# Softmax passes of a graph network: one product per tile with three bf16 parts side by side, in place of three products that accumulate

## The reference

```python
logits = leaky_relu(al_s[src] + al_d[dst], 0.2)
m = segment_max(logits, dst)
e = exp(logits - m[dst])
denom = segment_sum(e, dst)
alpha = e / denom[dst]
out = segment_sum(alpha[:, :, None] * xw[src], dst)
```

## Time and profile before

| | |
|---|---|
| median of 3 runs | 10558.96 us (10516.83 to 10563.09) |
| the profiled execution, its own time | 10553.33 us |
| its span, first to last instruction | 10551.6 us |
| mean granted TensorE clock | 0.627 of full speed |
| the three softmax passes lie at about | 4185 to 5770, 5870 to 7420, 7600 to 9010 us |

### The profile page before, as it was taken

One profiled execution on the slowest core, in us unless ns is written; L12 is line 12 of the kernel. 1 busy time (PEld: TensorE's weight loads), 2 busy tenths in 40 slices (PEclk: granted clock), 3 DMA queues, 4 the chain that ended last, 5 costly groups with the idle time before them and its releaser, 6 DMA issues. The chain is left out here.

```text
span 10551.6 us, 128176 instructions
## 1 busy us (share of the span) xinstructions
PE 5587.4 (53%) x36650; PEld 4424.0 (42%) x36651; DVE 3907.8 (37%) x11738; ACT 1797.2 (17%) x4681; POOL 5548.3 (53%) x5840
## 2 busy tenths in 40 slices
PE   3555555555544344665666565666545454545554
PEld 3444554444322222444444344444334443444444
DVE  4333322222311112554555455555444444333323
ACT  1222210100111112111111211111211111111111
POOL 3666656666366563554543454555355555255554
PEclk7555555656666666666667666666655555566665
DMA  3444422333232232433432443443223332233333
GB/s 112 144 143 141 143 69 75 80 78 78 57 75 73 72 74 68 114 112 108 115 110 80 118 113 110 112 113 109 64 79 83 79 82 77 63 97 97 98 96 80
DMA packets 711652, 1000.35 MB, mean 95 GB/s; under 512 B 355976, under 2 KB 397000, under 8 KB 711240
## 3 DMA queue, kind: packets, MB, share of 16 engines
q1 hardware_dynamic: 497816, 538.69, 17.4%
q0 software_dynamic: 213552, 458.86, 17.4%
HBM read 927.44 MB, written 69.60 MB: 94 GB/s over the span
## 5 line engine op out<-in xcount | busy, mean ns | idle before, releaser
L749 POOL DMA_INDIRECT gat_rows<-xw_table,gat_index x2496 | 2357.8, 945 | 2547.2 <-DVE gat_msg_s L1849 1442.7
L1948 PE MATMUL bank<-gat_msg_s,gat_hot 128*128 128x264 f32 (+1 forms) x4992 | 1898.5, 539 | 551.5 <-DVE acc L1870 213.6
L1948 PEld LDWEIGHTS bank<-gat_msg_s,gat_hot 128*128 128x128 f32 x4992 | 1289.7, 299 | 1020.1 <-issue 483.6
L749 POOL DMA_INDIRECT att_rows<-pre_table,att_index x832 | 784.9, 943 | 744.0 <-ACT att_index L739 349.1
L749 POOL DMA_INDIRECT msg_rows<-pre_table,msg_index x832 | 786.3, 945 | 610.8 <-ACT msg_index L739 369.8
L749 POOL DMA_INDIRECT gcn_rows<-x_table,gcn_index x832 | 806.4, 969 | 497.0 <-issue 260.0
L749 POOL DMA_INDIRECT gcn_rows<-in_x,gcn_index x832 | 804.9, 967 | 499.1 <-issue 252.9
L958 PE MATMUL bank<-gcn_rel,gcn_rhot 100*128 100x64 f32 x3328 | 638.9, 344 | 793.6 <-issue 618.4
L798 PE MATMUL bank<-gcn_msg_s,gcn_hot 128*128 128x128 f32 x3328 | 731.8, 373 | 426.9 <-issue 416.6
L958 PEld LDWEIGHTS bank<-gcn_rel,gcn_rhot 100*128 100x128 f32 x3328 | 614.0, 267 | 818.8 <-issue 714.5
L798 PEld LDWEIGHTS bank<-gcn_msg_s,gcn_hot 128*128 128x128 f32 x3328 | 640.3, 276 | 495.8 <-issue 495.7
(11 more groups left out here) (302 smaller groups left out, 8929.5 us busy)
## 6 DMA issues: line engine op xcount, KB each, us to landing
gcn_ids<-rel_rows SPq DMA_DIRECT2D x208, 400.0 KB
gat_hot_half<-edge_hots SPq DMA_DIRECT2D x312, 256.0 KB
gat_dhot<-dst_hots SPq DMA_DIRECT2D x312, 256.0 KB
gcn_dst<-dst_rows SPq DMA_DIRECT2D x104, 512.0 KB
gat_rows<-xw_table,gat_index POOLq DMA_INDIRECT x2496
edge_hots<-gcn_hot_half SPq DMA_DIRECT2D x104, 256.0 KB
dst_hots<-gcn_dhot SPq DMA_DIRECT2D x104, 256.0 KB
gcn_hot_half<-edge_hots SPq DMA_DIRECT2D x104, 256.0 KB
```

The source lines that it names most:

```text
L749: pool.indirect_dma_start(self.rows[n.q][:, j, :], None, self.table, bass.IndirectOffsetOnAxis(ap=self.index[n.q][:, j:j + 1], axis=0))\
L1948: ins = pe.matmul(bank_of(n, g)[:, 0:wide], hot[n.q][:, j, :], msg[q][:, j, :], start=j == n.groups[g].start, stop=j == n.groups[g].stop - 1)
```

## The change

In each softmax step, `pick` and `dst_gather` issue one product per tile instead of three. The three parts stand side by side in the moving operand, so that a product has 27 (pick) or 48 columns (dst_gather) and does not accumulate. The three results lie side by side in PSUM, and VectorE sums them with a `tensor_reduce` each: `found` (192 elements per partition in, 64 out) in `maxima`, and `drow` (384 in, 128 out) in `logits`. Both results now lie in SBUF, where before the sum was read from PSUM. The PSUM banks are free again once these sums are made: `pick` waits for `merged` (the sum of the step before) instead of `offered`, `dst_gather` for `joined` instead of `shifted`. `cut_ends` writes the third part as fp32 with a bf16 value in it, instead of as bf16. Tiles, gathers, loads and the orders of the engines stay.

```diff
-        ends, ends_rest = (ring_sb(st, s, TWO, [P, BATCH, HEADS + 1]) for s in ("ends_s", "ends_rest"))
-        ends_low = ring_sb(st, "ends_low", TWO, [P, BATCH, HEADS + 1], BF16)
+        cuts = ring_sb(st, "ends_s", TWO, [P, BATCH, PARTS, HEADS + 1])
+        ends, ends_rest, ends_low = ([t[:, :, k, :] for t in cuts] for k in range(PARTS))
+        found, merged = ring_sb(st, "found", TWO, [P, BATCH, HEADS]), st.sem("merged")
...
-        drow = row_ps[:, 0:BATCH * 2 * HEADS].rearrange("p (b h) -> p b h", b=BATCH)
+        drow, joined = ring_sb(st, "drow", TWO, [P, BATCH, 2 * HEADS]), st.sem("joined")
...
+        all_upper = lambda t: t.bitcast(BF16).rearrange("p b k (h two) -> p b (k h) two", two=2)[:, :, :, 1]
...
                     dve.wait_ge(picked, n.total(1, RING + 1))
-                    dve.tensor_scalar(pen[q][:, :].unsqueeze(2), view[:, :, HEADS:HEADS + 1], -1.0, -FAR, ALU.add, ALU.mult)\
+                    dve.tensor_scalar(pen[q][:, :].unsqueeze(2), view[:, :, 0, HEADS:HEADS + 1], -1.0, -FAR, ALU.add, ALU.mult)\
                         .then_inc(penal, 1)
+                    dve.tensor_reduce(found[q][:, :, :], view[:, :, :, 0:HEADS].rearrange("p b k h -> p b h k"), AX.X, ALU.add)\
+                        .then_inc(merged, 1)
+                    dve.wait_ge(merged, n.total(1, 1))
                     dve.wait_ge(penal, n.total(1, 1))
-                    dve.tensor_tensor(cand[q][:, :, :], view[:, :, 0:HEADS], spread(pen[q][:, :], HEADS), ALU.add)\
+                    dve.tensor_tensor(cand[q][:, :, :], found[q][:, :, :], spread(pen[q][:, :], HEADS), ALU.add)\
...
                     dve.wait_ge(dst_rows, n.total(1, RING + 1))
-                    dve.tensor_tensor(lg[q][:, :, :], al_s[q][:, :, :], drow[:, :, 0:HEADS], ALU.add)\
+                    dve.tensor_reduce(drow[q][:, :, :], row_ps[:, 0:BATCH * PARTS * 2 * HEADS]
+                                      .rearrange("p (b k h) -> p b h k", b=BATCH, k=PARTS), AX.X, ALU.add).then_inc(joined, 1)
+                    dve.wait_ge(joined, n.total(1, 1))
+                    dve.tensor_tensor(lg[q][:, :, :], al_s[q][:, :, :], drow[q][:, :, 0:HEADS], ALU.add)\
...
-                    pe.wait_ge(offered, n.total(1, 1))
-                    pieces = upper(ends[q][:, :, :]), upper(ends_rest[q][:, :, :]), ends_low[q]
+                    wait_past(pe, merged, n.total(1, 0))
+                    size = PARTS * (HEADS + 1)
+                    pieces = all_upper(cuts[q][:, :, :, :])
                     for j in range(BATCH):
-                        for k, piece in enumerate(pieces):
-                            ins = pe.matmul(pick_ps[:, j * (HEADS + 1):(j + 1) * (HEADS + 1)], hots.half[n.q][:, j, :], piece[:, j, :],
-                                            start=k == 0, stop=k == PARTS - 1)
+                        ins = pe.matmul(pick_ps[:, j * size:(j + 1) * size], hots.half[n.q][:, j, :], pieces[:, j, :],
+                                        start=True, stop=True)
                     ins.then_inc(picked, 1)
...
-                    size = 2 * HEADS
+                    size = PARTS * 2 * HEADS
                     pe.wait_ge(dhot_in[n.q], n.count(16, 16))
                     pe.wait_ge(shown, n.total(1, 1))
                     pe.wait_ge(parted, n.total(1, 1))
-                    pe.wait_ge(shifted, n.total(1, 1))
+                    wait_past(pe, joined, n.total(1, 0))
                     for j in range(BATCH):
-                        for k in range(PARTS):
-                            ins = pe.matmul(row_ps[:, j * size:(j + 1) * size], dhot[n.q][:, j * P:(j + 1) * P],
-                                            parts[q][:, n.group_at[j], k, :], start=k == 0, stop=k == PARTS - 1)
+                        ins = pe.matmul(row_ps[:, j * size:(j + 1) * size], dhot[n.q][:, j * P:(j + 1) * P],
+                                        parts[q][:, n.group_at[j], :, :].rearrange("p k h -> p (k h)"), start=True, stop=True)
                     ins.then_inc(dst_rows, 1)
```

More of the change, by code:

```diff
@@ L1755, in power @@
                     q = n.of(TWO)
-                    act.wait_ge(shifted, n.total(1, 2))
+                    act.wait_ge(shifted, n.total(1, 1))
                     act.wait_ge(msg_made, n.total(1, RING))
@@ L1792, in maxima @@
                     q = n.of(TWO)
-                    view = pick_ps[:, 0:BATCH * (HEADS + 1)].rearrange("p (b h) -> p b h", b=BATCH)
+                    view = pick_ps[:, 0:BATCH * PARTS * (HEADS + 1)].rearrange("p (b k h) -> p b k h", b=BATCH, k=PARTS)
                     first = n.turn is None and n.total(1, 0) == 0
@@ L1841, in logits @@
                     dve.wait_ge(leaky, n.total(1, 1))
-                    dve.tensor_tensor(lg[q][:, :, :], lg[q][:, :, :], drow[:, :, HEADS:2 * HEADS], ALU.subtract)\
+                    dve.tensor_tensor(lg[q][:, :, :], lg[q][:, :, :], drow[q][:, :, HEADS:2 * HEADS], ALU.subtract)\
                         .then_inc(shifted, 1)
@@ L1889, in _ @@
                 dve.sem_inc(offered, 1)
-                dve.sem_inc(shifted, 1)
                 dve.sem_inc(logit, TWO)
```

## The result

The changed kernel takes 10,860.66 us (median; 10,851.18 to 10,878.9), the kernel before in the same comparison 10,551.97. The ratio is 1.0298, 95% interval [1.0277, 1.0319]: slower by 3.0%, where 9880 us had been forecast.

The account below looks back on a forecast made before the run. VectorE's serial chain, waiting on TensorE's late `dst_rows`, was taken to bound the kernel. 10553 - 1005 (shorter wait) + 322 (two reductions) = 9870 us, 9876 for the median, given as 9880; range 9460 to 10,300.

Parts of the forecast that it names:

- The step that failed: Before the adds (line 1870): the wait for `summed`, 242.8 us, could be late next and was left as it was.
- My own reading: Softmax steps: while GpSimd gathers, TensorE's instruction supply and signals are slow, and a signal behind many short instructions comes late.
- The wait for `dst_rows`: Before `logits`: delay falls to one third with the products ahead; 371 us of 1376 stay, 1005 us removed.
- all of the wait goes: Rival, before `logits`: queued instructions cover the burst, the signal is prompt, the whole 1376 us go; 9505 us, chance 0.17.
- The reductions: VectorE's serial chain: two added reductions, 387 and 566 ns, 1.03 us a step with dependent starts, 322 us in all.
- the gather sets it (slower): Rival, softmax steps: `dst_rows` comes 1.7 us after the gathers' end whatever the products, 190 us more; 10,750 us, chance 0.09.
- The rival by the whole stream: Rival, TensorE: the delay goes with all its products, 35 of 67 kept, 723 us go; 10160 us, chance 0.20.
- The rule beside it: TensorE: about 62 ns per matmul, so 32 fewer products give 2.0 us a step, about 10,260 us.
- The 31 ns of my reading: TensorE: 24 pairs of product and weight load in 0.75 us, 31 ns each.
- the "issue" pauses in `pick`: TensorE in `pick`: some 650 us of pauses, off VectorE's path, expected to be nearly gone.
- 12.5 us: Softmax passes: a step falls by 2.2 us to 12.5, as the first two edge passes take.
- The sign of failure: Wrong if the `dst_rows` wait stayed over 900 us, like waits moved elsewhere, or PSUM reductions took well over 0.7 us each.

Follow-up runs that it names:

- 51 products in a step: Kernel before with only `dst_gather` or only `pick` merged, GpSimd also waiting for the sums of five steps ago: 0.9493 and 1.0092 of the kernel before.
- gated: The changed kernel, with GpSimd also waiting, before it gathers, for the sums of five steps ago: 10,064.07 us, 0.9451 of the kernel before.
- pick alone: Kernel before with only `pick` merged (one reduction of 192 elements in `maxima`), `dst_gather` keeping 24 products: 8072.9 us, 0.9986 of the kernel before.
- set 1: Runs timed together in which the kernel before took 8082.8 us.
- set 2: Runs timed together, kernel before 10,640.4 us; with plain loads for the softmax gathers, the changed kernel took 8964.01 us, the kernel before 8959.51.

## Why the prediction was wrong

**The step that failed** is in the part on what is moved: "`summed` would be late next: 242.8 us of 'remote' before line 1870, which I leave as it is", and with it "a microsecond less of that wait is a microsecond less of the step, until something else ends last". The next thing to end last was the same hold-back, one signal further on. I subtracted 1005 us for a wait that did shrink, by 1280 (1376.2 to 96.7), and added nothing for `summed`, which took 1372 us more (242.8 to 1614.9).

**What stayed unseen** is what a prompt `dst_rows` sets off. It ends the messages sooner, messages free a buffer, and GpSimd, until then stopped once a step, gathers for two steps on end. My own reading said that signals are late while GpSimd gathers; it should have been applied to all signals of TensorE and to the longer row.

**The wait for `dst_rows`:** 371 us forecast, 96.7 found, so the delay does not go in proportion to the products ahead. The rival "all of the wait goes" had this number nearly right and the time wrong (9505), for the same omission.

**The reductions:** 387 and 566 ns forecast, 346 and 556 found. By the PSUM formula of the Trainium skill's page "VectorE: DVE Perf Modes" (section on the TRN2 errata) the two take 0.85 us, an estimate; the trace has 0.90. What they cost was mis-sized by the overlap and not by the duration: 322 us forecast, some 115 found, as in the rows of 16 VectorE's chain keeps GpSimd waiting once for two steps. Added to the kernel before they cost 132 us (1.28%).

**The rival "the gather sets it (slower)"** had the sign and the size (10,750), but put the hold-back on `dst_rows`; it was on `summed`. Its sum had 190 us for one reduction a step and not the 331 us of longer passes, so that its number lies near is luck. Its chance of 0.09 was too low: its own evidence, 11 of 20 steps with the signal 1.7 us after the gathers, was evidence for any signal.

**The rival by the whole stream** fell: at 51 products in a step, the waits were 2.5 and 1782.5 us, by what stood ahead of `dst_rows`. The rule beside it, some 62 ns per matmul with hardware decoding off (the Trainium skill, "TensorE: Matmul & The Clock Gate", section on the 56 ns gap), is not borne out as a price here: products with their own weight loads start 26 ns apart within a burst (median, 16 columns, kernel before). The 31 ns of my reading had the last product's duration in it.

**What held:** the "issue" pauses in `pick` are nearly gone (639 us to 59), and the other passes are unchanged. A step comes near 12.5 us once GpSimd is gated (12.9), but with 811 us of wait for `summed` and 59 for `dst_rows` where 243 and 371 had been counted, so that does not bear the sum out. The sign of failure was named: "a wait of like size moved to `summed`".

**What stays open:** why TensorE's signals are held back while GpSimd gathers, why only in some sets of runs on the same chips, and how many products a signal may stand behind (8 passed, 24 did not; `summed`, held back in the changed kernel too, comes behind the 8 of `dst_gather`, the 8 of `pick` and its own). The hold-back and its condition are shown; its mechanism inside the chip is not.

## What to carry to other kernels

When a wait is put down to a condition (here: TensorE's signals while GpSimd gathers), ask of every later signal under the same condition before counting the wait as won. And ask what an earlier signal sets loose: an engine that may run ahead by several buffers will, and one added wait that holds it to a step was worth 8% of the changed kernel (1.0298 to 0.9451). Time the kernel before beside each set of runs: it moved by a quarter between sets here (10,666 to 8078 us), and the verdict with it.

## What the runs showed of the hardware

- While GpSimd issued indirect gathers, TensorE's completion was often seen only after the last gather of a row, although the products are recorded as done: 1.7 us after it in the kernel before (median, rows of 8), 2.0 us in the changed kernel with the gate (rows of 8), 3.1 us in the changed kernel (rows of 16), there up to 15.6 us after VectorE began to wait. Not in every step: of 268 waits over 1.5 us for `dst_rows` in the kernel before, 83 ended while gathers still followed. With plain loads issued by SyncE in their place there was no such wait.
- The same kernel took 8078 to 8083 us in two sets of runs and 10,552 to 10,666 in the others, on the same chips. One gather took the same in both (0.945 to 0.947 us); what differed was the waiting for signals. It shows outside the softmax passes too: before the gathers of the second edge pass, which no kernel here changes, GpSimd was idle for 313.1 us (pick alone, set 1) against 497.0. The mean granted clock was 0.69 in the quicker sets and 0.63 before, but 0.67 with plain loads in set 2 as well, so it may as well follow from the shorter waits; which way round was not tried.
- Within a burst, bf16 products with their own weight loads start 25 ns apart in the median where the granted clock is full (2.4 GHz) and 27 where it is half (1.2 GHz), for 9, 16 and 27 columns alike. For 48 columns it is 25 and 40 ns. So at the full clock three times the columns cost no more time.
- A reduction reading PSUM took 346 ns for 192 elements per partition and 556 for 384.
